# Second layer of a four-layer graph kernel: damping factor in a PSUM bank, logits in one PSUM bank, edge part added by VectorE

## The chip, the cores and the metric

One Trainium2 chip, one of its NeuronCores. The metric is the device time of one execution of the whole program in microseconds. The kernel before was run three times: 2078.06, 2093.66 and 2092.9 us, median 2092.9.

## The reference

Four graph layers run on 3125 nodes with 64 features and 53125 edges, sorted by their target. In front of each layer stands a layer norm with relu, behind it a residual addition. Layers are numbered 0 to 3 in the code; the change is in layer 1, an attention over the edges of a target:

```python
d = jax.nn.gelu(layer_norm(x @ Wd1 + bd1, g1, b1), approximate=False)
d = jax.nn.gelu(layer_norm(d @ Wd2 + bd2, g2, b2), approximate=False)
w2 = features @ W2
w3 = features @ W3
logits = w1[target] - w2[source] + d
seg_max = jax.ops.segment_max(logits, target, num_segments=m)
e = jnp.exp(logits - seg_max[target])
denom = jax.ops.segment_sum(e, target, num_segments=m)
a = e / denom[target]
out = jax.ops.segment_sum(a * (w3[source] + d), target, num_segments=m)
```

The term `w1[target]` is the same for all edges of a target and so drops out of the softmax. The kernel leaves it out of the logits (it is used only where a target's edges cross the seam between the two halves).

## The kernel before, in words

**Tiling.** The edge list is cut into two halves of 26624 edges, one on partitions 0 to 63, the other on 64 to 127 (a partition is a feature). A chunk is 512 edges of each half, a tile of 128 x 512 fp32. There are 52 chunks, `c`, and `k = c % 2` picks the slot of two-slot buffers. Segment sums are running scans along the edges, with a factor `keep` (uint8) that is 0 at the first edge of a target. Layer 1 needs three scans per chunk: the running maximum `mrun`, and, damped whenever the maximum rises, the running sum of weights `srun` and of weighted values `orun`.

**Where rows come from.** For 44 of the 52 chunks the rows -w2 and w3 of the source nodes come by gathers: GpSimd issues eight indirect DMAs per chunk (L609), one per group of 128 edges, each reading its 128 row numbers from the SBUF table `idx`. ScalarE copies them apart (`l1_split`, L1219) into `wsplit`. For the other 8 chunks (7, 13, ... 49, every sixth) TensorE makes the rows from one-hot matrices (L916), ScalarE copies a quarter (L1255) and VectorE picks the others (L1704). The gather ring `Gring` and `wsplit` have two slots: gathers of the g-th gathered chunk wait for the split of the one two before.

**A chunk on each engine, in program order.** Nothing is reordered; each engine follows its own list and waits on semaphores.

- TensorE, for chunk c: `l1_out_m(c)` turns `mrun` back to edges by rows (L860, four transposes); `l1_logits(c+1)` makes the logits of the next chunk, d by a product with the identity (L876, one product, which the trace shows as two passes), then -w2 added onto it by four products with the identity (L881, eight passes) or one product with W2 (L886); `l1_out(c-1)` turns both sums (L868); `l1_values(c)` makes w3 + d in PSUM bank 1 (L894, L898 or L901); behind it, behind four of six chunks, 10 or 16 one-hot products (L916).
- VectorE: `l1_max(c)`: maximum scan (L1734), then the three subtractions (L1738, L1739, L1740); `l1_sums(c-1)`: the damping factor (L1746), the scan of weights (L1751), weights times values (L1754), the scan of values (L1757). In two of six chunks three picks (L1704) follow.
- ScalarE: the exponential of both parts of `soft` (L1271), the split of c+1, the mask for c+2 (L1210), one-hot tiles (L1230, L1235), three evacuations (L1192).
- SyncE loads d of a chunk from DRAM into `dch` (three slots) when the values of the chunk three before are made, and stores the scans.

Logits alternate between PSUM banks 0 and 7. The damping factor lies in the first half of `soft[k]`, in SBUF.

Of the kernel before, what the change touches and what calls it, by code (L numbers as in the profile page):

```python
# [72 lines left out]
def build(nc, T, out):  # L73
    ctx = ExitStack()
    with ctx:
# [5 lines left out]
        def S(name, slot=None):  # L81
# [8 lines left out]
            "L0 msg made": 1, "L1 w2 transposed": 1, "L1 split": 1,   # L90
            "damp made": 1, "diff made": 1,  
            "ea product made": 1, "ea transposed": 1, "eaT copied": 1, "eu made": 1,
# [54 lines left out]
        def n_in_transposed(layer, n):  # L147
            return n_chunks((0, 1, None, 2)[layer], n)
# [231 lines left out]
        def _(sp):  # L380
# [131 lines left out]
            for c in range(NCH):  # L512
                if c + 3 < NCH:
                    sp.wait_ge(S("in transposed", c % 2), n_in_transposed(1, c // 2 + 1))
                    load_d(c + 3)
                if c:
                    l1_store((c - 1) // 2, (c - 1) % 2)
                if c + 3 in MULTIPLIED[1] and MULTIPLIED[1].index(c + 3) + 2 < len(MULTIPLIED[1]):
                    load_rows(1, MULTIPLIED[1].index(c + 3) + 2)
                if c in MULTIPLIED[1] and MULTIPLIED[1].index(c) + 2 < len(MULTIPLIED[1]):  # L520
                    load_quarters(1, MULTIPLIED[1].index(c) + 2)
# [150 lines left out]
        def _(pe):  # L672
# [198 lines left out]
            def l1_logits(c):  # L871

                k, bank = c % 2, 7 * (c % 2)
                pe.wait_ge(S("d loaded", c % 3), 16 * (c // 3 + 1))
                pe.wait_ge(S("diff made", k), past(c // 2))
                nc.tensor.matmul(P[:, bank, :], ident[:, :], dch[c % 3], start=True, stop=True)  # L876
                if c in FETCHED[1]:
                    g = FETCHED[1].index(c)
                    pe.wait_ge(S("L1 split", g % 2), past(g // 2 + 1))
                    for j in range(J):  # L880
                        last = nc.tensor.matmul(P[:, bank, j::J], wsplit[g % 2][:, j * 128:(j + 1) * 128], ident[:, :],  # L881
                                                start=False, stop=True, skip_group_check=True)
                else:
                    m = MULTIPLIED[1].index(c)
                    pe.wait_ge(S("L1 quarters picked", 1), m + 1)
                    last = nc.tensor.matmul(P[:, bank, :], W[:, W2NEG, :], rows[m % 2], start=False, stop=True,  # L886
                                            skip_group_check=True)
                last.then_inc(S("L1 w2 transposed", k), 1)

            def l1_values(c):  # L890

                k = c % 2
                pe.wait_ge(S("eu made", 1 - k), past(c // 2 + k))
                nc.tensor.matmul(P[:, 1, :], ident[:, :], dch[c % 3], start=True, stop=True)  # L894
# [514 lines left out]
        def _(dve):  # L1409
# [316 lines left out]
            def l1_max(c):  # L1726

                i, k = c // 2, c % 2
                logits = P[:, 7 * k, :]
                dve.wait_ge(S("m transposed", k), past(i))  # L1730
                dve.wait_ge(S("diff made", 1 - k), past(i + k))
                dve.wait_ge(S("L1 w2 transposed", k), past(i + 1))
                dve.wait_ge(S("neg made", k), past(i + 1))
# [8 lines left out]
            def l1_sums(c):  # L1742
                i, k = c // 2, c % 2
                damp, num = soft[k][:, 0:CH], soft[k][:, CH:2 * CH]
                dve.wait_ge(S("expd made", k), past(i + 1))
                v.scalar_tensor_tensor(damp, damp, 1.0, keep[:, at(i, k)], ALU.min, ALU.mult) \  # L1746
                    .then_inc(S("damp made", k), 1)
                dve.wait_ge(S("damp made", k), past(i + 1))
                dve.wait_ge(S("scanned", 1 - k), n_scanned(1, i + k))
                dve.wait_ge(S("out transposed", k), n_out_transposed(1, i))  # L1750
# [207 lines left out]
```

## Time and profile before

| | us |
|---|---|
| median of three runs | 2092.9 |
| the profiled execution | 2089.63 |
| its span in the profile | 2087.9 |
| GpSimd busy in the span | 1390.2 (67%) |
| TensorE busy | 1574.6 (75%) |
| VectorE busy | 1519.1 (73%) |
| ScalarE busy | 901.3 (43%) |

The profile is one execution. Busy time counts an engine's own instructions; idle time costs only if the engine is on the chain that ends last. In the rows, PE is TensorE, PEld its weight loads, DVE VectorE, ACT ScalarE, POOL GpSimd; L609 is line 609 of the kernel. TensorE's clock is the share of full speed that was granted, of two levels, 1.2 and 2.4 GHz. Names are tensors: `gathered` is the gather ring, `arena` one large SBUF tensor that holds all the work tiles of layer 1 (d, soft, the runs), `psum` the eight banks.

### The profile page before, as it was taken

The page shows a single profiled execution, that of the slowest core. Times are in us where ns is not written, and L with a number is a line of the kernel's source. Part 1 is how long each engine was busy: PE and PEld are TensorE (multiplying, and loading weights), DVE is VectorE, ACT ScalarE, POOL GpSimd, SP SyncE. Part 2 cuts the span into 40 slices and gives each one's busy share as a digit, 9 for nine tenths or more (in the row PEclk, how much of TensorE's full clock was granted, in tenths as well). Part 3 has the DMA queues.
Part 4 walks back from the last instruction along what each step waited for, and adds up shares of the span by engine and source line. Part 5 has one row for each costly group of instructions (what it writes and reads, how often), then busy time and mean ns, then how long its engine had stood idle before and what let it go on. Part 6 is the DMA issues. An engine that isn't in the chain of part 4 may idle for free. (4 is left out here: it accounts for less than half of the span.)

```text
span 2087.9 us, 24015 instructions
## 1 busy us (share of the span) xinstructions
PE 1574.6 (75%) x7395; PEld 1202.0 (58%) x7395; DVE 1519.1 (73%) x2399; ACT 901.3 (43%) x1184; POOL 1390.2 (67%) x1404
## 2 busy tenths in 40 slices
PE   2777877777566787888787169999987529999990
PEld 1555555555454665666565157777764317878880
DVE  6777767777674677777786677777768658999992
ACT  1333333333226676776753125555537413444430
POOL 5777777777637777777774557777750317777764
PEclk9966766667567999999998579999995559999995
DMA  5422223223223555554553424444455313434332
GB/s 125 109 77 82 82 72 87 73 81 86 67 56 103 159 167 157 157 175 157 168 168 128 107 61 93 99 94 94 93 109 189 107 24 75 102 93 113 94 94 52
DMA packets 216475, 220.63 MB, mean 106 GB/s; under 512 B 107230, under 2 KB 170163, under 8 KB 216115
## 3 DMA queue, kind: packets, MB, share of 16 engines
q1 hardware_dynamic: 167603, 147.32, 23.6%
q0 software_dynamic: 45024, 58.36, 13.4%
q10 hardware_dynamic: 3744, 13.63, 1.7%
q8 instruction: 58, 0.95, 0.2%
q14 instruction: 46, 0.38, 0.1%
HBM read 117.72 MB, written 101.46 MB: 105 GB/s over the span
## 5 line engine op out<-in xcount | busy, mean ns | idle before, releaser
L609 POOL DMA_INDIRECT gathered<-table,idx x1272 | 1271.6, 1000 | 511.3 <-issue 397.2
L1704 DVE COPY_PREDICATED spare<-spare,psum 64x512 f32<-64x512 uint8 x294 | 216.6, 737 | 117.5 <-ACT spare L1318 108.0
L964 PE MATMUL psum<-rounded 128*128 128x512 f32 x1144 | 272.7, 395 | 22.1 <-DVEq L1697 22.1
L964 PEld LDWEIGHTS psum<-rounded 128*128 128x128 f32 x1144 | 212.9, 189 | 65.6 <-DVEq L1697 22.5
L642 POOL DMA_INDIRECT arena<-scan,rowidx x100 | 104.8, 1048 | 152.5 <-DMA scan<-ea 94.5
L1734 DVE TENSOR_TENSOR_SCAN arena<-arena,psum 128x512 f32<-128x512 f32 x52 | 66.3, 1275 | 151.1 <-PE psum L881 150.6
L1318 ACT ACTIVATE spare<-psum 64x512 f32<-64x512 f32 x82 | 48.3, 590 | 295.6 <-PE psum L964 295.1
L1113 ACT ACTIVATE arena<-psum 128x1024 f32<-128x1024 f32 x52 | 53.2, 1024 | 242.5 <-PE psum L732 149.4
L881 PE MATMUL psum<-ident,arena 128*128 128x128 f32 x352 | 63.9, 338 | 99.0 <-ACT arena L1219 99.0
L1716 DVE TENSOR_SCALAR_CACHE_REDUCE rounded<-spare,rowcol 128x1024 fp32r<-128x1024 uint16 x110 | 134.4, 1269 | 0.2
L881 PEld LDWEIGHTS psum<-ident,arena 128*128 128x128 f32 x352 | 55.5, 238 | 133.6 <-ACT arena L1219 129.7
L746 PE MATMUL psum<-ident,arena 128*128 128x128 f32 x416 | 99.9, 386 | 40.3 <-DVE arena L1550 20.2
L746 PEld LDWEIGHTS psum<-ident,arena 128*128 128x128 f32 x416 | 68.4, 196 | 94.1 <-issue 48.6
L964 PE MATMUL psum<-rounded_keep 128*128 128x512 f32 x456 | 121.4, 415 | 0.0
L1559 DVE TENSOR_TENSOR arena<-gathered,wgt 128x512 f32<-128x512 f32 x52 | 36.2, 697 | 114.6 <-DMA gathered<-table,idx 114.6
L754 PE MATMUL psum<-ident,arena 128*128 128x128 f32 x208 | 51.1, 393 | 90.0 <-DVE scan_ring L1567 59.7
L740 PEld LDWEIGHTS psum<-W,arena 128*128 128x128 f32 x416 | 105.6, 329 | 5.6
L1192 ACT ACTIVATE arena<-psum 128x512 f32<-128x512 f32 x156 | 82.4, 595 | 61.1 <-PE psum L868 56.0
L740 PE MATMUL psum<-W,arena 128*128 128x128 f32 x416 | 101.8, 407 | 0.0
L964 PEld LDWEIGHTS psum<-rounded_keep 128*128 128x128 f32 x456 | 85.3, 190 | 25.6 <-issue 9.1
L754 PEld LDWEIGHTS psum<-ident,arena 128*128 128x128 f32 x208 | 33.5, 197 | 104.8 <-issue 64.7
L732 PE MATMUL psum<-Wd,arena 25*128 25x512 f32 x104 | 92.2, 1034 | 0.8 <-ACT arena L1109 0.8
(273 smaller groups left out, 3512.0 us busy)
## 6 DMA issues: line engine op xcount, KB each, us to landing
scan<-arena SPq DMA_DIRECT2D x52, 768.0 KB, 4.7
scan<-ostage SPq DMA_DIRECT2D x130, 256.0 KB, 2.2
gathered<-table,idx POOLq DMA_INDIRECT x1272
d_mlp<-arena ACTq DMA_DIRECT2D x26, 512.0 KB, 2.7
arena<-d_mlp SPq DMA_DIRECT2D x52, 256.0 KB, 3.1
ea<-in_edge_attr SPq DMA_DIRECT2D x104, 128.0 KB
spare<-src_row SPq DMA_DIRECT2D x98, 128.0 KB, 3.6
spare<-src_quarter SPq DMA_DIRECT2D x98, 96.0 KB, 3.0
```

What stands on the lines that cost most here:

```text
L609: pool.indirect_dma_start(out=out[:, j, hf, :], out_offset=None, in_=tab[layer], in_offset=bass.IndirectOffsetOnAxis(ap=idx[:, j, hf * NCH ...
L642: pool.indirect_dma_start(out=agg[:, b * width:(b + 1) * width], out_offset=None, in_=segs[layer], in_offset=bass.IndirectOffsetOnAxis(ap= ...
L732: last = nc.tensor.matmul(P[:, k, :], x3t[0:X3 + 1, k * 128:(k + 1) * 128], Wd1[:, :, :].rearrange("p r d -> p (r d)"), start=True, stop=True)
L740: last = nc.tensor.matmul(P[:, 2 + k, j * 128:(j + 1) * 128], y1[k][:, j::J], W[:, WD2, :], start=False, stop=True, skip_group_check=True)
L746: last = nc.tensor.transpose(P[:, 4, j::J], mlp[layer][:, k * CH + j * 128:k * CH + (j + 1) * 128], ident[:, :])
L754: last = nc.tensor.transpose(P[:, 5, j::J], msg[k][:, j * 128:(j + 1) * 128], ident[:, :])
L881: last = nc.tensor.matmul(P[:, bank, j::J], wsplit[g % 2][:, j * 128:(j + 1) * 128], ident[:, :], start=False, stop=True, skip_group_check ...
L964: last = nc.tensor.matmul(P[:, bank + t, :], parts[layer][n][:, b:b + 2, :].rearrange("p b d -> p (b d)"), tile(layer, m, u)[:, hf * CH:(h ...
L1192: return nc.scalar.activation(ostage1[k][:, :, :, n * D:(n + 1) * D].rearrange("p h j d -> p j h d"), P[:, 2 + n, :].rearrange("p (j h d) ...
L1704: picked = v.copy_predicated(rows[m % 2][halves[hf], :], quarter[m % 2][halves[hf], q - 1, :], P[halves[q % 2], bank + q // 2, :])
L1716: v.tensor_scalar(tile(layer, m, u), rowb[m % 2], rowcol[:, 0, u:u + 1], None, ALU.is_equal, ALU.add, accum_out=small[:, 6, NB + u:NB + u ...
L1734: v.tensor_tensor_scan(mrun[k], neg[k], logits, mrun[1 - k][:, CH - 1:CH], ALU.add, ALU.max) \
```

## The change

The factor is written to PSUM bank 7 by the same instruction that wrote it into SBUF, and both sum scans read it there. All logits use bank 0. TensorE puts only -w2 there: four transposes for a gathered chunk, or one product that starts the bank. VectorE then adds d from `dch` onto it in place, at the head of `l1_max`. For the values TensorE adds d as before. Waits follow: TensorE's logits of a chunk wait for the subtraction of the chunk directly before, the load of d also for the addition. In the new file, L880 are the transposes, L1730 the addition, L1735 the maximum scan, L1748 the factor, L1752 and L1758 the sum scans.

```diff
@@ -88,7 +88,7 @@
 
         ring_unit = {
             "L0 msg made": 1, "L1 w2 transposed": 1, "L1 split": 1, 
-            "damp made": 1, "diff made": 1,  
+            "damp made": 1, "diff made": 1, "logits made": 1,  
             "ea product made": 1, "ea transposed": 1, "eaT copied": 1, "eu made": 1,
             "evacuated": 1, "expd made": 1, "hidden made": 1, "hidden summed": 1,
             "L2 scan stored": 16, "d stored": 16, "in transposed": 1,
@@ -511,6 +511,7 @@
 
             for c in range(NCH):
                 if c + 3 < NCH:
+                    sp.wait_ge(S("logits made", c % 2), past(c // 2 + 1))
                     sp.wait_ge(S("in transposed", c % 2), n_in_transposed(1, c // 2 + 1))
                     load_d(c + 3)
                 if c:
@@ -870,26 +871,23 @@
 
             def l1_logits(c):
 
-                k, bank = c % 2, 7 * (c % 2)
-                pe.wait_ge(S("d loaded", c % 3), 16 * (c // 3 + 1))
-                pe.wait_ge(S("diff made", k), past(c // 2))
-                nc.tensor.matmul(P[:, bank, :], ident[:, :], dch[c % 3], start=True, stop=True)
+                k = c % 2
+                pe.wait_ge(S("diff made", 1 - k), past(c // 2 + k))
                 if c in FETCHED[1]:
                     g = FETCHED[1].index(c)
                     pe.wait_ge(S("L1 split", g % 2), past(g // 2 + 1))
                     for j in range(J):
-                        last = nc.tensor.matmul(P[:, bank, j::J], wsplit[g % 2][:, j * 128:(j + 1) * 128], ident[:, :],
-                                                start=False, stop=True, skip_group_check=True)
+                        last = nc.tensor.transpose(P[:, 0, j::J], wsplit[g % 2][:, j * 128:(j + 1) * 128], ident[:, :])
                 else:
                     m = MULTIPLIED[1].index(c)
                     pe.wait_ge(S("L1 quarters picked", 1), m + 1)
-                    last = nc.tensor.matmul(P[:, bank, :], W[:, W2NEG, :], rows[m % 2], start=False, stop=True,
-                                            skip_group_check=True)
+                    last = nc.tensor.matmul(P[:, 0, :], W[:, W2NEG, :], rows[m % 2], start=True, stop=True)
                 last.then_inc(S("L1 w2 transposed", k), 1)
 
             def l1_values(c):
 
                 k = c % 2
+                pe.wait_ge(S("d loaded", c % 3), 16 * (c // 3 + 1))
                 pe.wait_ge(S("eu made", 1 - k), past(c // 2 + k))
                 nc.tensor.matmul(P[:, 1, :], ident[:, :], dch[c % 3], start=True, stop=True)
                 if c in FETCHED[1]:
@@ -1726,10 +1724,13 @@
             def l1_max(c):
 
                 i, k = c // 2, c % 2
-                logits = P[:, 7 * k, :]
+                logits = P[:, 0, :]
+                dve.wait_ge(S("d loaded", c % 3), 16 * (c // 3 + 1))
+                dve.wait_ge(S("L1 w2 transposed", k), past(i + 1))
+                v.tensor_tensor(logits, logits, dch[c % 3], ALU.add).then_inc(S("logits made", k), 1)
+                dve.wait_ge(S("logits made", k), past(i + 1))
                 dve.wait_ge(S("m transposed", k), past(i))
                 dve.wait_ge(S("diff made", 1 - k), past(i + k))
-                dve.wait_ge(S("L1 w2 transposed", k), past(i + 1))
                 dve.wait_ge(S("neg made", k), past(i + 1))
                 v.tensor_tensor_scan(mrun[k], neg[k], logits, mrun[1 - k][:, CH - 1:CH], ALU.add, ALU.max) \
                     .then_inc(S("m scanned", k), 1)
@@ -1741,12 +1742,12 @@
 
             def l1_sums(c):
                 i, k = c // 2, c % 2
-                damp, num = soft[k][:, 0:CH], soft[k][:, CH:2 * CH]
+                damp, num = P[:, 7, :], soft[k][:, CH:2 * CH]
                 dve.wait_ge(S("expd made", k), past(i + 1))
-                v.scalar_tensor_tensor(damp, damp, 1.0, keep[:, at(i, k)], ALU.min, ALU.mult) \
+                dve.wait_ge(S("scanned", 1 - k), n_scanned(1, i + k))
+                v.scalar_tensor_tensor(damp, soft[k][:, 0:CH], 1.0, keep[:, at(i, k)], ALU.min, ALU.mult) \
                     .then_inc(S("damp made", k), 1)
                 dve.wait_ge(S("damp made", k), past(i + 1))
-                dve.wait_ge(S("scanned", 1 - k), n_scanned(1, i + k))
                 dve.wait_ge(S("out transposed", k), n_out_transposed(1, i))
                 v.tensor_tensor_scan(srun[k], damp, num, srun[1 - k][:, CH - 1:CH],
                                      ALU.mult, ALU.add).then_inc(S("s scanned", k), 1)
```

VectorE's list in a chunk before (a row is line, operation, result<-inputs and shape of the result; scans print as SCALAR_TENSOR_TENSOR; in brackets the semaphores waited for):

```order
L1734 SCALAR_TENSOR_TENSOR arena<-arena,psum 128x512 [waits L1_w2_transposed_1,neg_made_1,diff_made_0,m_transposed_1]
L1738 TENSOR_TENSOR arena<-arena 128x1 [waits scanned_1,m_scanned_1]
L1739 TENSOR_TENSOR arena<-arena 128x511
L1740 TENSOR_TENSOR arena<-psum,arena 128x512
L1746 SCALAR_TENSOR_TENSOR arena<-arena,keep 128x512 [waits expd_made_0]
L1751 SCALAR_TENSOR_TENSOR arena<-arena 128x512 [waits out_transposed_0,scanned_1,damp_made_0]
L1754 TENSOR_TENSOR arena<-arena,psum 128x512 [waits in_transposed_0]
L1757 SCALAR_TENSOR_TENSOR arena<-arena 128x512 [waits s_scanned_0,eu_made_0]
```

The same chunk of the changed kernel:

```order
L1730 TENSOR_TENSOR psum<-psum,arena 128x512 [waits L1_w2_transposed_1,d_loaded_1]
L1735 SCALAR_TENSOR_TENSOR arena<-arena,psum 128x512 [waits diff_made_0,neg_made_1,m_transposed_1,logits_made_1]
L1739 TENSOR_TENSOR arena<-arena 128x1 [waits scanned_1,m_scanned_1]
L1740 TENSOR_TENSOR arena<-arena 128x511
L1741 TENSOR_TENSOR arena<-psum,arena 128x512
L1748 SCALAR_TENSOR_TENSOR psum<-arena,keep 128x512 [waits scanned_1,expd_made_0]
L1752 SCALAR_TENSOR_TENSOR arena<-psum,arena 128x512 [waits out_transposed_0,damp_made_0]
L1755 TENSOR_TENSOR arena<-arena,psum 128x512 [waits in_transposed_0]
L1758 SCALAR_TENSOR_TENSOR arena<-psum,arena 128x512 [waits s_scanned_0,eu_made_0]
```

One instruction is new at the head, and the maximum scan waits for it. The two sum scans now have `psum` among their inputs, and the factor has it as its result.

TensorE's list between two chunks before (a gathered chunk with 10 one-hot products behind the one in front, cut to the logits and their neighbours):

```order
L860 MATMUL psum<-ident,arena 128x128 [waits m_evacuated_0,m_scanned_1]
L860 MATMUL psum<-ident,arena 128x128 x3
L876 MATMUL psum<-arena,ident 128x512 [waits diff_made_0,d_loaded_2]
L881 MATMUL psum<-ident,arena 128x128 [waits L1_split_0]
L881 MATMUL psum<-ident,arena 128x128 x3
L868 MATMUL psum<-ident,arena 128x128 [waits evacuated_1,scanned_0]
L868 MATMUL psum<-ident,arena 128x128 x7
L894 MATMUL psum<-arena,ident 128x512 [waits eu_made_0]
```

And in the changed kernel:

```order
L861 MATMUL psum<-ident,arena 128x128 [waits m_evacuated_0,m_scanned_1]
L861 MATMUL psum<-ident,arena 128x128 x3
L880 MATMUL psum<-ident,arena 128x128 [waits L1_split_0,diff_made_1]
L880 MATMUL psum<-ident,arena 128x128 x3
L869 MATMUL psum<-ident,arena 128x128 [waits evacuated_1,scanned_0]
L869 MATMUL psum<-ident,arena 128x128 x7
L892 MATMUL psum<-arena,ident 128x512 [waits eu_made_0,d_loaded_1]
```

The product with d (L876) is gone from the logits; its wait for `d loaded` has gone to the values. The wait on `diff made` names the other slot, the chunk just before.

## Rows read from the trace of the kernel before

**Rows 1.** The page's part 4: the chain that ended last, by engine, by line

```profile
POOL 19%; PE 10%; DVE 8%; issue 7%; DMA 2%; ACT 1%; DVEq 0%; POOLq 0%; SPq 0%; ACTq 0%
POOL gathered L609 16%; PE psum L964 8%; DVE scan_ring L1867 3%; POOL arena L642 3%; PE psum L1054 1%; DMA gathered<-table,idx 1%; DVE scan_ring L1912 1%; DVE arena L1800 1%; DMA arena<-scan,rowidx 0%; PE psum L1064 0%; DMA table<-arena 0%; DVE arena L1445 0%; DVE arena L1444 0%; DVE arena L1449 0%; DVE small L1442 0%
```

**Rows 2.** Timeline of GpSimd: first gather, first lengthened, longest gap, last

```profile
626.84 0.94 POOL L609 DMA_INDIRECT gathered<-table,idx  x1 [29.45 <-DMA table<-arena]
...
643.06 1.35 POOL L609 DMA_INDIRECT gathered<-table,idx  x1 [0.30 <-issue]
...
949.17 0.94 POOL L609 DMA_INDIRECT gathered<-table,idx  x1 [5.48 <-issue]
...
1130.26 1.60 POOL L609 DMA_INDIRECT gathered<-table,idx  x1 [0.31 <-issue]
```

**Rows 3.** Busy by stretch: stretch, length, five engines, clock, DMA share, GB/s

```profile
626.80:1131.90 505.10, 395.05 (x1928) 296.62 (x1928) 355.87 (x452) 325.27 (x422) 387.26 (x352) 0.91 0.50 156
...
200.00:500.00 300.00, 233.50 (x1092) 168.73 (x1092) 216.87 (x421) 99.24 (x136) 226.80 (x241) 0.67 0.28 79
```

**Rows 4.** Waits, 626.8 to 1132 us: who for whom, us in total, times, longest

```profile
DVE arena L1734 <- PE psum L881: 144.8, 31, 20.2
PEld psum L881 <- ACT arena L1219: 123.6, 35, 11.1
POOL gathered L609 <- issue: 117.8, 351, 5.5
```

**Rows 5.** Groups on GpSimd, second layer, then first: busy us, mean ns | idle

```profile
L609 POOL DMA_INDIRECT gathered<-table,idx x352 | 387.3, 1100 | 147.2 <-issue 117.8 <-DMA table<-arena 29.4
...
L609 POOL DMA_INDIRECT gathered<-table,idx x327 | 310.8, 951 | 116.7 <-issue 99.3 <-DMA table<-arena 17.3
```

**Rows 6.** Timeline of GpSimd, 903 to 914 us: start us, duration us

```profile
903.57 1.55 POOL L609 DMA_INDIRECT gathered<-table,idx  x1 [0.30 <-issue]
...
906.67 0.94 POOL L609 DMA_INDIRECT gathered<-table,idx  x1 [0.30 <-issue]
...
910.41 1.64 POOL L609 DMA_INDIRECT gathered<-table,idx  x1 [0.31 <-issue]
912.36 1.60 POOL L609 DMA_INDIRECT gathered<-table,idx  x1 [0.30 <-issue]
```

**Rows 7.** Timeline of VectorE, 903 to 914 us

```profile
903.08 1.28 DVE L1757 TENSOR_TENSOR_SCAN arena<-arena 128x512 f32<-128x512 f32 x1
904.40 2.28 DVE L1704 COPY_PREDICATED spare<-spare,psum 64x512 f32<-64x512 uint8 x3
906.71 1.28 DVE L1734 TENSOR_TENSOR_SCAN arena<-arena,psum 128x512 f32<-128x512 f32 x1
...
908.10 0.68 DVE L1739 TENSOR_TENSOR arena<-arena 128x511 f32<-128x511 f32 x1
...
909.30 0.68 DVE L1746 SCALAR_TENSOR_TENSOR arena<-arena,keep 128x512 f32<-128x512 f32 x1
910.02 1.28 DVE L1751 TENSOR_TENSOR_SCAN arena<-arena 128x512 f32<-128x512 f32 x1
...
911.92 1.28 DVE L1757 TENSOR_TENSOR_SCAN arena<-arena 128x512 f32<-128x512 f32 x1
913.12 1.25 DVE L1734 TENSOR_TENSOR_SCAN arena<-arena,psum 128x512 f32<-128x512 f32 x1
```

**Rows 8.** Groups of VectorE and TensorE, 626.8 to 1143 us

```profile
L1740 DVE TENSOR_TENSOR arena<-psum,arena 128x512 f32<-128x512 f32 x52 | 35.6, 684 | 0.0
L1739 DVE TENSOR_TENSOR arena<-arena 128x511 f32<-128x511 f32 x52 | 35.6, 684 | 0.0
...
L1754 DVE TENSOR_TENSOR arena<-arena,psum 128x512 f32<-128x512 f32 x51 | 33.8, 662 | 0.0
...
L881 PE MATMUL psum<-ident,arena 128*128 128x128 f32 x352 | 63.9, 338 | 99.0 <-ACT arena L1219 99.0
...
L876 PE MATMUL psum<-arena,ident 128*128 128x512 f32 x104 | 54.8, 609 | 3.0 <-DMA arena<-d_mlp 3.0
```

**Rows 9.** Timeline, 888 to 898 us, chunk behind a one-hot chunk

```profile
888.37 1.23 PE L868 MATMUL psum<-ident,arena 128*128 128x128 f32 x8 [0.57 <-DVE arena L1757]
...
894.91 0.63 PE L860 MATMUL psum<-ident,arena 128*128 128x128 f32 x4
...
896.25 1.05 PE L881 MATMUL psum<-ident,arena 128*128 128x128 f32 x8
...
897.87 1.28 DVE L1734 TENSOR_TENSOR_SCAN arena<-arena,psum 128x512 f32<-128x512 f32 x1 [3.18 <-PE psum L881]
```

## The prediction

> **What bounds the kernel now.** I read the chain of work that ended last first [rows 1]. GpSimd has the largest share of it, 19%, and 16% are the gathers of L609. TensorE has 10%, VectorE 8%. The change touches only the second layer, so the next view is the busy time in that stretch. The 352 gathers of the layer begin at 626.8 us and the last is over at 1131.9 us [rows 2]: 505 us for 52 chunks, and no engine is full in it [rows 3]. GpSimd is busy for 387 us, but its idle time is 118 us in 351 pieces whose releaser is "issue" [rows 4]. That is the 0.30 us between two gathers, which it pays whatever happens. So GpSimd waits for nobody, apart from three longer gaps (2.2, 4.0 and 5.5 us, the longest in [rows 2]), each 112 gathers after the one before and with no releaser. VectorE does wait: L1734, the scan of the maximum, stands idle 145 us for TensorE's L881, and L881 stands behind L1219, ScalarE's split of the gathered rows, which needs the gather. The stage runs at the gathers' pace.
>
> **What sets that pace.** A gather takes 1100 ns on average here and 951 ns in the first layer [rows 5]; the short ones take 0.94 us in both. 352 x (1100 - 944) ns = 55 us is the lengthening. The two timelines, laid beside each other, show its cause [rows 6, 7]. The gather at 910.41 ends at 912.05, 0.75 us after the scan L1751 (910.02 to 911.30). The one at 912.36 ends at 913.96, 0.76 us after L1757 (911.92 to 913.20). The one at 903.57 ends 0.76 us after the L1757 of 903.08. The gather at 906.67 starts just before the scan L1734, of the same length, and takes 0.94 us. L1751 and L1757 read both inputs from SBUF; L1734 has one in PSUM. Going through all 352 gathers in this way, 91 are lengthened (first and last in [rows 2]): 49 end behind L1757, 27 behind L1751, 15 behind L1739, also with two SBUF inputs. They make 30.6, 19.9 and 4.6 us, together 55.1, which is all of it. None ends behind L1734, L1740, L1754 or the picks L1704, which have PSUM inputs. So two VectorE scans hold the bounding engine up for 50.5 us.
>
> **The change, part by part.**
> *The damping factor in PSUM.* Both sum scans now read one SBUF and one PSUM input. I take it that they stop holding gathers up: L1740 has its first input in PSUM and its second in SBUF, as the new scans do, and lengthens nothing. Worth 50.5 us at most. The writer of the factor now writes PSUM; no row shows VectorE doing that. The nearest, L1740 and L1754, read it and take 684 and 662 ns, L1739 without PSUM 684. Bounds: 0 to +0.6 us a chunk (a doubled pass), and I take 0.
> *What stays.* L1739 and the factor's own instruction (L1746 now) keep two SBUF inputs. Gathers now drift against VectorE instead of being caught behind the scans, so more will meet these two. A start-to-start of 1.25 us against about 0.6 us of L1739 in each of 52 chunks gives 52 x 0.6 / 1.25 = 25 meetings of 0.3 us, 7.5 us. As much again if L1746 holds too; [rows 7] has no case of it. I take 12 us, with 4 and 16 as ends.
> *The addition on VectorE.* 52 instructions, one input PSUM, one SBUF, result in place. By L1740 0.68 us, and since the scan waits for its end about 0.72 us: 37 us more VectorE work. Back to back a chunk takes 906.71 to 913.12 = 6.41 us now [rows 7]; it becomes 7.13. Twice in six chunks there are three picks of 2.28 us. Six chunks: 6 x 7.13 + 2 x 2.28 = 47.3 us. In six chunks five are gathered: 40 x 1.25 = 50 us of GpSimd. The addition is covered by VectorE's idle time at L1734, with 3 us of six chunks to spare. Without cover it would cost all 37.
> *TensorE.* It loses L876, 104 passes in two per chunk, 55 us [rows 8]. L881's 352 passes (two per product) become 176 single ones. L860, four transposes of this size, takes 0.63 us where L881's eight take 1.05 [rows 9]. Off TensorE: about 1.5 us a chunk, 80 us in all. It was waiting for splits anyway, so this gains nothing by itself; it pays for the next point.
> *One logits bank.* The product for chunk c+1 waits for the subtraction of chunk c. TensorE has just waited for the scan in front of that subtraction and has done L860 (0.63 us); the subtraction ends 1.4 us after the scan. Worst case 0.7 us a chunk, 36 us, with the column sums, values and one-hot products queued behind it. Where the gather is late, nothing. Where TensorE is late, as in [rows 9] (VectorE idle 3.18 us behind one-hot products, L860, L876, L881), it comes to L881 long after the subtraction, and the 1.5 us taken off pay for the addition twice. The waits put on the loads of d and on the factor's bank are for things done earlier in the same order: nothing.
>
> **The Trainium skill, beside this.** By "SBUF — State Buffer", section "Who interferes with whom", a VectorE instruction with two SBUF inputs contends with a GpSimd one that reads SBUF, and the loser blocks for the whole instruction; the trace agrees, and by this rule L1746 would hold too (the 16 us end). The same section also says of `tensor_tensor` that it did not stall DMAs, since descriptor generation needs the write interface (marked as inferred). By that sentence nothing is freed, and the second rival below would be the result. L1739's 15 lengthened gathers speak against it.
>
> **Sum.** Gather phase now: 352 x 0.944 + 351 x 0.305 + 10.8 (the three gaps beyond their 0.3) + 55 = 505. After: 332.3 + 107.1 + 10.8 + 12 = 462. Then there is a cost of two engines being near each other: VectorE's 47.3 and GpSimd's 50 us plus about 3 of holds and gaps, with two ring slots between them. A fall of TensorE's clock, now 0.91 of full on average, puts TensorE behind for a chunk, and GpSimd then waits for a split. I estimate 5 us. 467, a gain of 38. The tail behind the last gather trades half of L881 for the addition, within 0.5 us. The profiled execution took 2089.6 us (span 2087.9), the median of the three runs is 2092.9, with one at 2078. 2089.6 - 38 = 2051.6; as a median of runs, one to two more: **2053 us**.
>
> **The rivals.**
> *1. Another loop takes the stage over.* The gathers are freed, but VectorE and TensorE can't do six chunks in 53 us. The loop is: column sums, values and up to 16 one-hot products, L860, logits, on TensorE (about 7.5 us at full clock, by the stretch from 888.4 to 897.3 in [rows 9] less 1.5), then addition, scan, differences and sums on VectorE (7.1). Two chunks take 14.6 us with one-hot products, so VectorE's own 47.3 is the larger, but each handoff and each slow stretch of TensorE adds. At 55.5 us for six chunks the stage is 52/6 x 55.5 = 481, gain 24: 2067. For: only 3 us of slack. Against: TensorE loses 80 us. Chance 17%.
> *2. Nothing freed.* The scans hold gathers up with their first input in PSUM too, or the gathers wait later for what they gained. Gather phase still 505: 2088 to 2092. For: no scan with that operand order is in the trace. Against: L1740. Chance 12%.
> *3. Slower, by TensorE's clock.* TensorE has fewer columns to do and waits longer. In the first layer, busy 0.78 of 300 us, its granted clock is 0.67 (between its levels of 1.2 and 2.4 GHz); in this stage, busy 0.78 too, 0.91 [rows 3]. If it fell to 0.67, its 395 - 80 = 315 us, 36 per six chunks, would grow by 0.91/0.67 to 49. With all of those 13 us in the loop (50.5 now: VectorE's 47.3 and about 3 of handoffs, my estimate), six chunks take 63.5 and the stage 550: 2135. It is slower by over 1% once ten of the 13 lie in the loop (52/6 x 60.7 = 526 us). Against: the one-hot products stay, and they are what runs longest without a pause. Chance 6%.
>
> **How the numbers follow.** The forecast has 65%, with its own range from 2040 (holds 4 us, no stalls) to 2062. With rival 1 up to 2078, 82% is covered; below, if the three gaps vanish too, 2036. Range 2036 to 2078. A measurement tells about 1% (21 us) from no change. Faster by over 1% (under 2072): the forecast and two thirds of rival 1, 0.77. Same: the rest of rival 1 and rival 2, 0.17. Slower 0.06.
>
> **What would show it.** The mean gather at L609 in this stage near 975 to 985 ns instead of 1100, and none ending 0.75 us behind a sum scan; a few behind L1740 and L1748 of the new file. The addition at 0.68 us; VectorE's idle at its head below 100 us. TensorE about 315 us busy in the stage. GpSimd's idle still nearly all in pieces of 0.30 us; longer pieces would mean rival 1. A mean of 1100 again would mean rival 2, a clock below 0.8 rival 3. The other layers should keep their lengths; a difference there would spoil the prediction.

## The result and the profile after

The changed kernel takes 2056.4 us (median of four runs, 2056.07 to 2058.85), the kernel before 2086.5 over its four runs (2078.06 to 2093.66). The ratio is given as 0.9866, with a 95% interval of 0.9841 to 0.9892 (the two medians alone give 0.9856): 1.3% faster, at a time of 2056 us against a forecast of 2053. The profiled execution took 2056.71 us (span 2054.7).

The page of the changed kernel, part 4, the chain that ended last (answers to [rows 1]), then two groups of its part 5 (the gathers over all four layers, and the addition):

```profile
POOL 16%; PE 16%; DVE 8%; issue 6%; DMA 2%; ACT 1%; DVEq 0%; POOLq 0%; SPq 0%; ACTq 0%
...
L610 POOL DMA_INDIRECT gathered<-table,idx x1272 | 1223.9, 962 | 517.1 <-issue 396.7
...
L1730 DVE TENSOR_TENSOR psum<-psum,arena 128x512 f32<-128x512 f32 x52 | 36.0, 692 | 69.0 <-PE psum L880 68.6
```

GpSimd's share of the chain fell from 19 to 16%, TensorE's rose from 10 to 16%. Most of the rise is L962, 13% where the same line (L964 before) had 8% [rows 1]; it runs only from 1181 us on, in the third and fourth layers, so these shares say little about the change. The stage itself is over sooner; here is its busy time (columns as in [rows 3]: stretch, length, busy us of TensorE, its loads, VectorE, ScalarE, GpSimd, then clock, DMA share, GB/s), with the first layer's stretch under it:

```profile
627.00:1089.50 462.50, 340.84 (x1652) 267.26 (x1652) 390.19 (x501) 326.86 (x424) 339.53 (x352) 0.85 0.55 170
200.00:500.00 300.00, 230.07 (x1083) 166.00 (x1082) 216.12 (x420) 99.21 (x135) 227.00 (x240) 0.69 0.29 79
```

The gathers of the layer now fill 461.8 us, from the first start to the last end (called the phase from here on), where they filled 505.0. GpSimd's busy time is down by 48 us, with the same 352 gathers. VectorE's is up by 34, TensorE's down by 54. The first layer's row is nearly as before.

The waits of that stage in the changed kernel (who for whom, us in total, times, longest; answers to [rows 4]):

```profile
POOL gathered L610 <- issue: 117.2, 347, 5.5
...
PE psum L880 <- ACT arena L1217: 92.8, 30, 13.7
DVE psum L1730 <- PE psum L880: 68.6, 24, 19.0
```

VectorE stands idle for TensorE for 69 us at the addition, where it stood 145 us at the maximum scan. Now the timelines that answer to [rows 6] and [rows 7]: GpSimd, then VectorE, of the changed kernel from 903 to 914 us.

```profile
904.39 0.94 POOL L610 DMA_INDIRECT gathered<-table,idx  x1 [0.30 <-issue]
...
911.89 0.94 POOL L610 DMA_INDIRECT gathered<-table,idx  x1 [0.31 <-issue]
913.13 0.94 POOL L610 DMA_INDIRECT gathered<-table,idx  x1 [0.30 <-issue]
...
944.93 1.44 POOL L610 DMA_INDIRECT gathered<-table,idx  x1 [0.30 <-issue]
```

```profile
904.29 1.28 DVE L1758 TENSOR_TENSOR_SCAN arena<-psum,arena 128x512 f32<-128x512 f32 x1
908.55 0.70 DVE L1730 TENSOR_TENSOR psum<-psum,arena 128x512 f32<-128x512 f32 x1 [2.98 <-PE psum L880]
909.28 1.28 DVE L1735 TENSOR_TENSOR_SCAN arena<-arena,psum 128x512 f32<-128x512 f32 x1
...
911.95 0.68 DVE L1748 SCALAR_TENSOR_TENSOR psum<-arena,keep 128x512 f32<-128x512 f32 x1
912.67 1.28 DVE L1752 TENSOR_TENSOR_SCAN arena<-psum,arena 128x512 f32<-128x512 f32 x1
...
944.87 0.68 DVE L1740 TENSOR_TENSOR arena<-arena 128x511 f32<-128x511 f32 x1
```

The gather at 904.39 begins inside the scan L1758, the one at 913.13 inside L1752; both take 0.94 us. In the kernel before, the three gathers of [rows 6] that began inside these two scans took 1.55, 1.64 and 1.60. 93 gathers of the layer begin inside one of the two, and none of them is lengthened by it. In the kernel before 100 did, and only 76 were lengthened: all that began between 0.1 and 1.08 us behind the scan's start, and none that began earlier or later. Of the 93 now, 70 begin in that part. What still holds gathers up is L1740, with two SBUF inputs: the gather at 944.93 ends at 946.37, 0.82 us after it. Counted over all 352: 22 gathers are lengthened by 7.2 us in all, 21 behind L1740 and one behind the factor L1748. Before it was 91 and 55.0 us.

### The profile page after: what moved, and what is told of

Same layout as the page of the kernel before. It is cut to its first block and busy times, and to the rows that moved or that the text cites. A ratio compares the mean times of both kernels' runs of the same rounds, so it can differ in the third digit from the quotient of the medians.

```text
span 2054.7 us, 23714 instructions
## 1 busy us (share of the span) xinstructions
PE 1516.0 (74%) x7115; PEld 1171.0 (57%) x7115; DVE 1555.7 (76%) x2451; ACT 902.2 (44%) x1184; POOL 1344.1 (65%) x1404
## 5 line engine op out<-in xcount | busy, mean ns | idle before, releaser
L610 POOL DMA_INDIRECT gathered<-table,idx x1272 | 1223.9, 962 | 517.1 <-issue 396.7
L962 PE MATMUL psum<-rounded 128*128 128x512 f32 x1144 | 273.2, 395 | 22.1 <-DVEq L1695 22.1
L962 PEld LDWEIGHTS psum<-rounded 128*128 128x128 f32 x1144 | 213.2, 189 | 65.8 <-DVEq L1695 22.5
L643 POOL DMA_INDIRECT arena<-scan,rowidx x100 | 106.5, 1065 | 159.9 <-DMA scan<-ea 102.3
L747 PE MATMUL psum<-ident,arena 128*128 128x128 f32 x416 | 100.7, 388 | 39.7 <-ACT arena L1107 19.9
L747 PEld LDWEIGHTS psum<-ident,arena 128*128 128x128 f32 x416 | 68.8, 197 | 94.2 <-issue 49.6
L962 PE MATMUL psum<-rounded_keep 128*128 128x512 f32 x456 | 121.5, 415 | 0.0
L755 PE MATMUL psum<-ident,arena 128*128 128x128 f32 x208 | 50.2, 387 | 91.8 <-DVE scan_ring L1565 61.5
L880 PE MATMUL psum<-ident,arena 128*128 128x128 f32 x176 | 32.2, 313 | 92.8 <-ACT arena L1217 92.8
L962 PEld LDWEIGHTS psum<-rounded_keep 128*128 128x128 f32 x456 | 85.3, 190 | 25.7 <-issue 9.1
L869 PE MATMUL psum<-ident,arena 128*128 128x128 f32 x416 | 74.1, 334 | 30.0 <-DVE arena L1758 30.0
L755 PEld LDWEIGHTS psum<-ident,arena 128*128 128x128 f32 x208 | 32.7, 194 | 107.1 <-issue 66.5
L1730 DVE TENSOR_TENSOR psum<-psum,arena 128x512 f32<-128x512 f32 x52 | 36.0, 692 | 69.0 <-PE psum L880 68.6
```

The lines of the kernel that those rows point to most:

```text
L610: pool.indirect_dma_start(out=out[:, j, hf, :], out_offset=None, in_=tab[layer], in_offset=bass.IndirectOffsetOnAxis(ap=idx[:, j, hf * NCH ...
L643: pool.indirect_dma_start(out=agg[:, b * width:(b + 1) * width], out_offset=None, in_=segs[layer], in_offset=bass.IndirectOffsetOnAxis(ap= ...
L747: last = nc.tensor.transpose(P[:, 4, j::J], mlp[layer][:, k * CH + j * 128:k * CH + (j + 1) * 128], ident[:, :])
L755: last = nc.tensor.transpose(P[:, 5, j::J], msg[k][:, j * 128:(j + 1) * 128], ident[:, :])
L869: last = nc.tensor.transpose(P[:, 3 + n, j * 128:(j + 1) * 128], run[:, j::J], ident[:, :])
L962: last = nc.tensor.matmul(P[:, bank + t, :], parts[layer][n][:, b:b + 2, :].rearrange("p b d -> p (b d)"), tile(layer, m, u)[:, hf * CH:(h ...
```

## What the experiments were to tell apart

**The theory (G, the gathers)**: the gain is that the two sum scans no longer hold gathers up, and it comes from the factor's place alone. **The first rival (T, TensorE)**: the gain is TensorE's relief, the 55 us product with d gone from the logits and half of L880's passes gone with it. **The second question**: is the addition on VectorE covered by idle time, as the forecast said? Four edits answer: the factor in PSUM without the addition (`damp_only`), the addition without the factor in PSUM (`add_only`), the single logits bank alone (`bank_only`), and one more VectorE instruction (`more_dve`). The first two keep the logits in one bank, as the changed kernel does. `damp_only` differs from the changed kernel in two things at once, VectorE's addition and TensorE's product, and so prices only the exchange of one for the other.

They ran on four chips. On three of them the kernel before itself takes 2624 to 2652 us instead of 2085, which shifts every number of those runs; they are read only against the kernel before on the same chip, in a section of their own. The runs `f_damp_only`, `f_add_only` and `k_more_dve` ran where the kernel before takes 2082 to 2085 us, as in the forecast, and the theory is judged by them.

## The factor in PSUM alone

The factor stays in PSUM and the logits in one bank; TensorE adds d again, and the addition and its waits are gone. Against the changed kernel:

```diff
 def l1_logits(c):
+    pe.wait_ge(S("d loaded", c % 3), 16 * (c // 3 + 1))
     pe.wait_ge(S("diff made", 1 - k), past(c // 2 + k))
+    nc.tensor.matmul(P[:, 0, :], ident[:, :], dch[c % 3], start=True, stop=True)
...
-            last = nc.tensor.transpose(P[:, 0, j::J], wsplit[g % 2][:, j * 128:(j + 1) * 128], ident[:, :])
+            last = nc.tensor.matmul(P[:, 0, j::J], wsplit[g % 2][:, j * 128:(j + 1) * 128], ident[:, :],
+                                    start=False, stop=True, skip_group_check=True)
...
 def l1_max(c):
-    v.tensor_tensor(logits, logits, dch[c % 3], ALU.add).then_inc(S("logits made", k), 1)
-    dve.wait_ge(S("logits made", k), past(i + 1))
```

> The same kernel as e_damp_only (factor in PSUM, TensorE adds d, no addition on VectorE). In the first call every kernel, that of before too (2629 us), had ScalarE and VectorE standing for some 10 to 15 us at a time without a releaser in the program, in all four layers; this run asks the same question where those stops are absent. Theory G: 25 to 35 us under the kernel before, mean gather 960 to 980 ns, GpSimd waiting for splits 5 to 15 us. Rival T: under 5 us of gain. If the stops are there again (kernel before above 2500 us), then as in the first call: 0 to 25 us over the kernel before, because the gathers are not what the stage waits for.

Measured: 2040.94 us (four runs, 2040.13 to 2046.57), before 2085.01, ratio 0.9784 (0.9765 to 0.9803). Its stage, then, in a second view, the gathers' group in a stretch that holds them all (line, operation, count, busy us, mean ns, idle time before by releaser):

```profile
627.00:1084.00 457.00, 376.81 (x1928) 281.18 (x1928) 355.61 (x452) 322.73 (x422) 339.16 (x352) 0.94 0.55 172
```

```profile
L609 POOL DMA_INDIRECT gathered<-table,idx x352 | 339.9, 966 | 146.9 <-issue 115.1 <-DMA table<-arena 29.7 <-ACT arena L1219 2.1
```

TensorE has all its 1928 matmuls again and VectorE its 452 instructions, and the gathers still take 966 ns. The lengthening is 7.7 us, the phase 457.2 us. So the gain needs neither TensorE's relief nor the addition. The phase is 47.8 us shorter than before, of which 47.3 are lengthening that is gone (55.0 to 7.7) and 0.5 shorter gaps, so nothing of it is left for the single bank to have gained or cost. This version is 2.2% faster than the kernel before, and its ratio lies below that of the changed kernel: it beats both.

## The addition without the factor in PSUM

```diff
 def l1_sums(c):
-    damp, num = P[:, 7, :], soft[k][:, CH:2 * CH]
+    damp, num = soft[k][:, 0:CH], soft[k][:, CH:2 * CH]
```

> The same kernel as e_add_only (factor in SBUF, one logits bank, VectorE adds d). Theory G: within 5 us of the kernel before, gather phase 500 to 510 us, 80 to 95 gathers lengthened. Rival T: 20 to 33 us under the kernel before.

Measured: 2090.04 us (ten runs), before 2085.01, ratio 1.0026 (1.0015 to 1.0037). Its stage, the gathers' group, and one gather and the scan that it ends behind, from the timelines of GpSimd and VectorE:

```profile
627.00:1122.00 495.00, 346.09 (x1652) 273.92 (x1652) 390.01 (x502) 328.62 (x424) 380.22 (x352) 0.83 0.51 159
```

```profile
L610 POOL DMA_INDIRECT gathered<-table,idx x352 | 381.1, 1083 | 142.5 <-issue 113.4 <-DMA table<-arena 29.1
```

```profile
721.30 1.55 POOL L610 DMA_INDIRECT gathered<-table,idx  x1 [0.30 <-issue]
```

```profile
720.81 1.28 DVE L1758 TENSOR_TENSOR_SCAN arena<-arena 128x512 f32<-128x512 f32 x1
```

The scan reads two SBUF inputs again (722.09 at its end) and the gather ends 0.76 us later (722.85), the delay of the kernel before. 96 gathers are lengthened, by 48.8 us. TensorE is relieved just as in the changed kernel (346 us busy in the stage, 1652 matmuls) and nothing is gained. Its gather phase is 10.5 us shorter than before (6.2 us less lengthening and 4.3 less in the gaps), and the stretches outside it give that back, 7.3 us of it between the third and fourth layers. This is the clean pair: this kernel and the changed one differ by where the factor lies, and in nothing else, and they stand 1.6% apart (0.9866 and 1.0026 of before; 34 us by the medians). Their phases differ by 32.7 us: 41.5 us less lengthening, less 8.8 us more of waits and gaps on GpSimd. Rival T falls.

## One more VectorE instruction

An in-place copy of the same size, ahead of the addition; all else is the changed kernel.

```diff
 def l1_max(c):
+    v.tensor_scalar(logits, logits, 1.0, None, ALU.mult).then_inc(S("logits copied"), 1)
+    dve.wait_ge(S("logits copied"), c + 1)
     v.tensor_tensor(logits, logits, dch[c % 3], ALU.add).then_inc(S("logits made", k), 1)
```

> The changed kernel with one more VectorE instruction of 0.7 us per chunk, a copy of the logits in place in PSUM ahead of the addition: 37 us more of VectorE work. On a chip like that of the changed kernel's own runs (kernel before near 2085 us). By the slack of the prediction: 2 to 10 us over the changed kernel, so 2058 to 2066. If the first addition already cost 10 to 15 us, as f_damp_only hints, the second finds less slack still: 15 to 30 us over it, 2071 to 2087, GpSimd waiting 30 us or more for splits. Never under it.

Measured: 2073.46 us (seven runs), before 2081.82, ratio 0.9960 (0.9944 to 0.9975). Two groups of its stage, then two of its waits:

```profile
L610 POOL DMA_INDIRECT gathered<-table,idx x352 | 338.5, 962 | 162.4 <-issue 106.9 <-DMA table<-arena 29.9 <-ACT arena L1217 25.6
...
L1730 DVE TENSOR_SCALAR psum<-psum 128x512 f32<-128x512 f32 x50 | 34.6, 692 | 50.7 <-PE psum L880 50.3
```

```profile
POOL gathered L610 <- issue: 106.9, 338, 2.1
...
DVE psum L1730 <- PE psum L880: 50.3, 20, 19.7
```

The view shows 50 of them; all 52 such instructions are 36 us, and the kernel is 17 us slower than the changed one by the medians (0.9960 and 0.9866 of before). The gathers are as short as there (962 ns), but GpSimd now stands idle 25.6 us behind the split L1217, where it was 5.0 us in four gaps of the changed kernel (0.68, 2.66, 0.85 and 0.84). Its phase is 471.0 us (461.8 there), and from its last gather to the next layer's first it takes 94.05 us (87.45). VectorE has 50 us of idle time left at its head, and yet half of the 36 us comes through. TensorE's clock is not the reason, being 0.86 in this stage (0.85 in the changed kernel's row above):

```profile
628.00:1100.00 472.00, 341.93 (x1632) 269.58 (x1632) 416.49 (x542) 322.51 (x417) 338.47 (x352) 0.86 0.52 163
```

The exchange of TensorE's product for the addition, one step earlier, cost about as much: the kernel with the addition stands at 0.9866 of before, the one with the product at 0.9784, 15.5 us by the medians and 17 by the ratios, with 36 us more work on VectorE. The two were measured beside different runs of before. In the profiles they are 9.9 us apart, 4.5 of it in the phase and 4.2 between it and the next layer, but the profiled execution without the addition was the slowest of its four, 5.6 us over their median. How much of this is the addition and how much TensorE's lower clock (0.85 against 0.94) no run separates; `k_more_dve` shows only that an instruction on VectorE alone can cost that much.

## The same kernels where the program takes 2.6 ms

The four edits first ran on a chip where the kernel before takes 2629 us. `bank_only` is the kernel before with this edit (and the same change in the lines that read the bank):

```diff
 def l1_logits(c):
-    k, bank = c % 2, 7 * (c % 2)
+    k = c % 2
     pe.wait_ge(S("d loaded", c % 3), 16 * (c // 3 + 1))
-    pe.wait_ge(S("diff made", k), past(c // 2))
-    nc.tensor.matmul(P[:, bank, :], ident[:, :], dch[c % 3], start=True, stop=True)
+    pe.wait_ge(S("diff made", 1 - k), past(c // 2 + k))
+    nc.tensor.matmul(P[:, 0, :], ident[:, :], dch[c % 3], start=True, stop=True)
```

> The changed kernel with d added to the logits by TensorE again (product with the identity, then eight passes), VectorE's addition gone; damping factor still in PSUM bank 7, logits still all in bank 0. Theory G (the whole gain is that the two sum scans no longer hold the gathers up): mean gather of the stage 960 to 980 ns, gather phase 462 to 475 us, time 25 to 35 us under the kernel before, since TensorE's extra 80 us lie mostly beside the gathers. Rival T (the gain comes from TensorE losing the product with d, which VectorE was waiting for): under 5 us of gain.

> The changed kernel with the damping factor back in SBUF: one logits bank and VectorE's addition stay. Theory G: 80 to 95 gathers lengthened again, mean about 1100 ns, gather phase 500 to 510 us, time within 5 us of the kernel before. Rival T: 20 to 33 us under it, with a mean gather near 1100 ns all the same.

> The kernel before with all logits in bank 0 and nothing else: TensorE adds d, the factor is in SBUF. Theory G: 0 to 3 us more than the kernel before, gather phase 503 to 510 us, since the extra wait for the subtraction lies beside the gathers. Rival W (one bank costs up to the 0.7 us a chunk of the prediction): up to 36 us more.

> The changed kernel with one more VectorE instruction per chunk, a copy of the logits in place in PSUM (times 1), for which the addition waits: another 0.72 us x 52 = 37 us of VectorE work that lengthens no gather. Theory G with the slack of the prediction (six chunks 47.3 us of VectorE against about 53 of gathers): VectorE at 51.6 us for six chunks, 2 to 10 us more than the changed kernel, and GpSimd's waits for splits up from 4 us. Rival B (VectorE's loop already binds in the changed kernel): 30 to 37 us more.

On a second such chip the changed kernel itself ran beside three of them, on a third the single bank once more:

> The changed kernel, beside the others on one chip. As measured before: 30 us under the kernel before (ratio 0.985 to 0.987), gather phase about 462 us, GpSimd's waits about 15 us.

> Factor in PSUM, TensorE adds d. Theory A (VectorE's addition costs on top: it puts VectorE, 0.72 us a chunk later, in front of the splits that gathers wait for, and of the stage's end): 8 to 15 us under g_after. Rival (the 15 us between the two were the chips): within 4 us of g_after.

> One logits bank and nothing else. Theory G: 0 to 3 us over the kernel before, gather phase 500 to 508 us. Rival W: 10 to 36 us over it (up to 0.7 us a chunk).

> The changed kernel with one more VectorE instruction of 0.7 us per chunk ahead of the addition (a copy of the logits in place, in PSUM), 37 us more of VectorE work. By the slack of the prediction (47.3 of 53 us) 2 to 10 us over g_after. If the second loop already shares the bound, as the cost of the first addition (f_damp_only against after) hints: 15 to 30 us over g_after, with GpSimd waiting 30 us or more for splits.

> The kernel before with all logits in one bank and nothing else. Theory G: the extra wait for the subtraction lies beside the gathers: 0 to 3 us over the kernel before, 85 to 95 lengthened gathers, mean near 1100 ns, gather phase 500 to 508 us. Rival W: up to 0.7 us a chunk, 10 to 36 us over it. Should it be under the kernel before by more than 5 us, the single bank itself would carry part of what f_damp_only gained.

Measured (the last three columns are of the second layer, counted from the traces as above; the kernel before took 2629.32 us beside the runs `e_`, 2624.01 beside `g_` and 2651.78 beside `k_bank_only`):

| run | us | ratio (95%) | mean gather, ns | phase, us | GpSimd waits in it, us |
|---|---|---|---|---|---|
| e_damp_only | 2653.3 | 1.0131 (1.0076, 1.0187) | 962 | 581.2 | 135.6 |
| e_add_only | 2630.8 | 1.0027 (0.9994, 1.0060) | 1041 | 556.2 | 83.0 |
| e_bank_only | 2613.4 | 0.9947 (0.9911, 0.9984) | 1065 | 562.7 | 80.8 |
| e_more_dve | 2664.6 | 1.0136 (1.0069, 1.0202) | 950 | 590.0 | 148.7 |
| g_after | 2639.0 | 1.0080 (1.0047, 1.0114) | 951 | 578.1 | 136.6 |
| g_damp_only | 2650.1 | 1.0108 (1.0065, 1.0151) | 955 | 595.1 | 152.0 |
| g_bank_only | 2610.7 | 0.9945 (0.9910, 0.9980) | 1068 | 565.7 | 82.7 |
| g_more_dve | 2671.1 | 1.0175 (1.0113, 1.0236) | 955 | 601.7 | 158.6 |
| k_bank_only | 2641.5 | 0.9988 (0.9957, 1.0020) | 1062 | 562.3 | 81.5 |

What these chips do differently shows best in the first layer, which the change doesn't touch. Waits from 100 to 600 us in `g_after`:

```profile
ACT arena L1111 <- remote: 230.7, 17, 16.4
PEld psum L747 <- ACT arena L1107: 196.3, 17, 14.2
...
POOL gathered L610 <- DVE arena L1557: 150.7, 17, 10.4
```

In the same stretch of the profile of the kernel before that the forecast was made from (span 2087.9 us):

```profile
ACT arena L1113 <- PE psum L732: 138.2, 22, 8.2
POOL gathered L609 <- issue: 110.3, 362, 0.3
```

Seventeen times in 500 us ScalarE stands for up to 16 us behind something that the profile calls remote, TensorE and VectorE stand behind ScalarE, and GpSimd behind VectorE. The counts show GpSimd held up like this in all four layers (206, 137, 128 and 67 us in `g_after`, against 0, 15.3, 0 and 0 in the changed kernel's own profile), so GpSimd no longer runs the stage at its own pace there.

No profile of the kernel before was taken on these chips, so the four kernels with the factor in SBUF stand in for it. What follows: the mechanism shows on these chips too. With the factor in PSUM the gathers take 950 to 962 ns in five runs, with it in SBUF 1041 to 1068 in four. But there it gains nothing; the five kernels with the factor in PSUM are 0.8 to 1.8% slower than the kernel before, and GpSimd waits 53 to 78 us longer in the phase than in the four others. A gather that is done sooner waits longer for the same slot, which would explain about 40 us of it and no longer phase. Why the phase gets longer by 12 to 45 us over the others, and what the stops are, stays open; no run here separates it. The single bank costs nothing there (0.9945, 0.9947, 0.9988). It was not measured alone where the kernel before takes 2085 us. The bound from there is `f_damp_only`, which has it and gains 44 us.

## Why the prediction was right, step by step

The mechanism was right. That the time came within 4 us of the forecast is in part luck. The forecast gain was 38 us (1.8%), the measured one 33 us in the profiles and 1.3% by the ratio. The time came close because two errors went opposite ways: the phase was forecast 5 us too long and the stretches outside it 10 us too short.

- **The bounding engine and its hold: right.** The step "two VectorE scans hold the bounding engine up for 50.5 us" is borne out by the pair that differs only in the factor's place: 48.8 us of lengthening with it in SBUF, 7.2 with it in PSUM, and 1.6% of the time. One of its readings was weak: the gather at 906.67, "just before the scan L1734", would have shown nothing, since gathers that begin just before L1751 take 0.94 us too. The counts carry the step: 25 gathers of the kernel before begin between 0.1 and 1.08 us into L1734 and none is lengthened, where all 76 at such places in L1751 and L1757 are.
- **What stays, 12 us (4 to 16): measured 7.2.** The forecast had 25 meetings of L1739 (L1740 in the new file) at 0.3 us; there were 21, and with the one below they make 22 of 0.33 us. The "as much again if L1746 holds too" did not come: L1748 holds, but 23 of the 24 gathers that begin inside it do so in its first 0.01 or last 0.1 us; the other is the one at 775.90 with 1.08 us (end 776.98, L1748's end 776.17). `f_add_only` has a second case, 1.36 us, ending 0.82 us behind it. By the Trainium skill, "SBUF — State Buffer", section "Who interferes with whom", it should hold, having two SBUF inputs; both cases agree. The section's other sentence, by which `tensor_tensor` was seen not to stall DMAs (the reason marked as inferred), does not hold for these gathers: L1740 lengthened 21 of them.
- **GpSimd's other waits, 10.8 + 5 us: measured 15.3.** The three gaps came again, before the same gathers (the 114th, 226th and 338th; 5.49, 2.14 and 4.75 us idle, where the kernel before had 2.19, 5.48 and 4.04); the four waits behind the split make 3.8 us beyond the usual 0.3. With them the phase is 461.8 us against 467 predicted. Against before it is 47.8 us less of lengthening and 4.5 us more of gaps and waits.
- **The addition: size right, cover wrong.** It takes 692 ns (forecast 0.68) and a chunk back to back takes 7.15 us, the shortest 7.12 (forecast 7.13). But "the addition is covered by VectorE's idle time at L1734, with 3 us of six chunks to spare" was too good: the kernel without it (and with the product on TensorE) is 15 to 17 us faster. Of that, 4.5 us lie in the phase and 4.2 us between it and the next layer, where the forecast's "tail behind the last gather", "within 0.5 us", was too small as well; the remainder is not located. The likely fault of the step is to compare sums over six chunks, 47.3 and 50 us: VectorE's 69 us of idle time are 24 pieces with one of 19 us among them, and a chunk in which VectorE has none would pay for the addition. No run counts this chunk by chunk, but the instruction added on top cost in the same two places, with the clock as it was: +9.2 us in the phase, +6.6 behind it. The phase as forecast came out nevertheless, since its 5 us for stalls were about what this took; they had been meant for two engines being near each other and a fall of TensorE's clock.
- **TensorE, 395 - 80 = 315 us: measured 341.** The 276 matmuls are gone, as said, but the rest ran at a granted clock of 0.85 instead of 0.91. With the product back and more work to do, the same stage had 0.94 in `f_damp_only`. So what rival 3 expected of the clock came in part: it fell, by 0.06 and not by 0.24, and the kernel was not slower. Whether the fall carries part of the 15 to 17 us above stays open.
- **Outside the stage: 0 predicted, +10 us measured.** The span is 33.2 us shorter where the phase is 43.3. The largest piece is 6.9 us between the third and fourth layers, from 170.8 to 177.7 us. The chain of waits shows it, in the changed kernel and in the two others of its kind here; first the kernel before, then the changed one:

```profile
1550.67 4.36 DMA gathered<-table,idx
```

```profile
1511.12 10.90 DMA gathered<-table,idx
```

It is the last gather of the third layer: the time from its start on GpSimd (1550.67 and 1511.12) to its rows being there. The prediction said that a difference in other layers would spoil it, and this took 7 us of it. `f_damp_only` (10.21), `f_add_only` (11.26) and `k_more_dve` (11.38) have it too, whatever the second layer looked like, so it needs neither the addition nor the factor in PSUM. All four have the single logits bank, which is thus not excluded, and the kernel before was profiled only once. Its cause is open. The rest is 0.9 us ahead of the stage, 1.3 us behind it, where the last chunk's addition lies open and the forecast had 0.5, and 1.5 us in the third layer, less 0.5 in the fourth.
- **The sum.** The profiled execution was forecast at 2051.6 us and took 2056.7: the phase 5 us shorter than forecast, the stretches outside it 10 us longer. The low end of the range does not follow from its terms: 2040 less the three gaps (10.8) is 2029, not 2036.

## What to carry to other kernels

Where indirect gathers bound a stage, look at which VectorE instructions they overlap before looking at their data: one operand of the long ones in PSUM freed 42 to 48 us of GpSimd's time here, with no instruction added. Then stop: the idle time of another engine is no free room, since one more VectorE instruction per chunk cost half its length while that engine still had 50 to 70 us idle. And measure on a second chip: the factor in PSUM (with the single bank, without the addition) gained 2.2% on one and lost 1.1 and 1.3% on two others.

## What was not expected of the hardware

- A held gather ends 0.75 us after the end of a scan, and 0.82 us after a `tensor_tensor` (0.81 and 0.82 after the factor's instruction, two cases), wherever in that instruction it began. Not every gather that begins inside is held: of 100 in the two sum scans of the kernel before, the 24 unheld ones began in the scan's first 0.08 us, or in its last 0.16, where a gather of 0.94 us would not be over sooner anyway.
- VectorE writing the factor to PSUM costs 692 ns against 0.68 us into SBUF, and adding in place in PSUM 692 ns: nothing doubled.
- TensorE was granted more clock with more to do in the same stage: 0.83 and 0.85, between its two levels of 1.2 and 2.4 GHz, with the product gone (`f_add_only`, changed kernel; 346 of 495 and 341 of 462 us busy), 0.94 with it (`f_damp_only`; 377 of 457 us). What sets this is not shown.
- GpSimd pauses 2 to 5.5 us before every 112th gather of the second layer with no releaser, at the same gathers in the kernels before and changed, `f_damp_only` and `f_add_only`. In `k_more_dve` the first of the three is 0.64 us, behind a wait of 3.51 for the split one gather earlier.
- On three of the chips the kernel before takes 26 to 27% longer, with stops of 10 to 16 us; the profile names no engine of this core for them.
